# Sixteen-head attention: key products behind the output products, two units ahead, and four small moves on the other engines

## What is computed

```python
q = (hidden_states @ Wq).reshape(B, Sq, H, D)           # H = 16 heads of D = 128, Sq = 512
k = (encoder_hidden_states @ Wk).reshape(B, Skv, H, D)  # Skv = 512, context width 256
v = (encoder_hidden_states @ Wv).reshape(B, Skv, H, D)
q, k = rmsnorm(q, gq), rmsnorm(k, gk)
attn = softmax(einsum('bqhd,bkhd->bhqk', q, k) * scale)
out = einsum('bhqk,bkhd->bqhd', attn, v).reshape(B, Sq, H * D) @ Wo
x = x + tanh(g_xattn[2]) * out
```

```python
def step(state, inp):            # 16 states per channel, 512 positions
    d, b, c, u = inp
    dA = jnp.exp(d[..., None] * A)
    state = state * dA + (d * u)[..., None] * b[:, None, :]
    return state, jnp.einsum('bdn,bn->bd', state, c)
```

## Time and profile before

| | |
|---|---|
| time, median of 3 runs | 3549.21 us (3537.89 to 3550.49) |
| the profiled execution's own time | 3549.66 us |
| its span, first to last instruction | 3547.6 us |
| mean granted TensorE clock | 0.957 |
| busy: PE, DVE, ACT, POOL | 88%, 74%, 51%, 40% of the span |

### The profile page before, as it was taken

How to read it: one execution, slowest core, us unless ns; L and a number is a source line. 1 busy time by engine, 2 the same in 40 slices (tenths; PEclk the granted TensorE clock), 3 DMA queues, 4 the chain that set the end, 5 groups by cost and what they waited for, 6 DMA issues and landing times. The chain is left out here.

```text
span 3547.6 us, 42725 instructions
## 1 busy us (share of the span) xinstructions
PE 3130.4 (88%) x14213; PEld 1831.5 (52%) x14244; DVE 2623.1 (74%) x3494; ACT 1801.9 (51%) x3414; POOL 1416.0 (40%) x956
## 2 busy tenths in 40 slices
PE   7869788999996888699999999999999777998985
PEld 3337544333333555455555555555555356786663
DVE  7855698877765888478777877787777764766886
ACT  5644343666653445465666566655555332664220
POOL 1122288000000000076777777767767544223440
PEclk9879999999998999999999999999999888999997
DMA  4137745222218300255555454445444346665321
GB/s 131 47 117 271 266 121 129 66 57 57 57 30 169 41 1 1 83 175 158 173 172 173 157 172 161 160 157 179 165 158 138 119 166 202 241 249 205 142 72 59
DMA packets 229748, 478.65 MB, mean 135 GB/s; under 512 B 36239, under 2 KB 69647, under 8 KB 213664
## 3 DMA queue, kind: packets, MB, share of 16 engines
q1 hardware_dynamic: 223296, 459.19, 40.9%
q0 software_dynamic: 6240, 16.81, 1.4%
HBM read 387.51 MB, written 92.06 MB: 135 GB/s over the span
## 5 line engine op out<-in xcount | busy, mean ns | idle before, releaser
L2378 POOL TENSOR_TENSOR l2x_inflow<-l2x_dtu,l2x_rows_b 128x512 f32<-128x512 f32 x256 | 419.4, 1638 | 271.2 <-DVE l2x_state L2267 263.0
L178 POOL TENSOR_TENSOR ln_work<-ln_work,minus_half 128x4 f32<-128x4 f32 (+1 forms) x34 | 33.2, 976 | 1037.4 <-DVE ln_work L166 1037.3
L2267 DVE TENSOR_TENSOR_SCAN l2x_state<-l2x_decay,l2x_inflow 128x512 f32<-128x512 f32 x256 | 383.1, 1497 | 16.8 <-ACT l2x_decay L2141 16.8
L1324 DVE TENSOR_REDUCE l1x_mx<-psum 128x2 f32<-128x1024 f32 x256 | 308.3, 1219 | 100.0 <-PE psum L1166 98.5
L2394 POOL TENSOR_TENSOR l2x_y_sum<-l2x_y_sum,l2x_state 128x512 f32<-128x512 f32 x224 | 354.4, 1582 | 33.0 <-DVE l2x_state L2276 33.0
L2076 ACT ACTIVATE l2x_probs<-psum,l2x_soft,l2x_norms 128x512 f32<-128x512 f32 x256 | 195.5, 775 | 320.2 <-DVE l2x_soft L2206 320.2
L1281 ACT ACTIVATE l1x_split<-psum 128x1024 f32<-128x1024 f32 x256 | 262.0, 1025 | 158.7 <-PE psum L1166 158.6
L2276 DVE TENSOR_TENSOR l2x_state<-l2x_state,l2x_rows_c 128x512 f32<-128x512 f32 x256 | 266.8, 1042 | 7.6 <-DMA l2x_rows_c<-l3x_xd_dram 1.1
L126 PE MATMUL psum<-l2x_probs_t,l2x_v_tok 128*128 128x512 f32 x512 | 236.3, 605 | 28.9 <-ACT l2x_probs_t L212 25.9
L126 PE MATMUL psum<-l2x_xt,l2x_wq 128*128 128x512 f32 x512 | 230.9, 594 | 7.7 <-issue 6.2
L126 PE MATMUL psum<-l2x_kt,l2x_qt 128*128 128x512 f32 x512 | 230.5, 593 | 4.0 <-ACT l2x_probs L2076 4.0
(11 more groups left out here) (458 smaller groups left out, 7199.6 us busy)
## 6 DMA issues: line engine op xcount, KB each, us to landing
l2x_rows_b<-l3x_xd_dram SPq DMA_DIRECT2D x256, 256.0 KB, 3.7
l2x_rows_c<-l3x_xd_dram SPq DMA_DIRECT2D x256, 256.0 KB, 3.7
l2w_raw<-l_w SPq DMA_DIRECT2D x38, 1024.0 KB, 7.0
l2x_wkv<-l2x_kv_dram SPq DMA_DIRECT2D x32, 1024.0 KB, 6.9
l2w_raw<-l_w SPq DMA_DIRECT2D x38, 512.0 KB, 4.5
l1x_heads_dram<-l1x_stage SPq DMA_DIRECT2D x32, 512.0 KB, 3.3
l2x_wq<-l_wq SPq DMA_DIRECT2D x16, 1024.0 KB, 7.2
l2x_wo<-l_wo SPq DMA_DIRECT2D x16, 1024.0 KB, 5.3
```

What stands on the lines that cost most here:

```text
L1324: main.drain(dve.tensor_reduce(mx[:, gg % 2, :, j, t], g["psum"][:, b:b + 2, :], AX.X, ALU.max), f"m{n}_0", banks=2)
L2267: dve.tensor_tensor_scan(state[:, s % KEPT, :], decay[:, s % 3, :], inflow[:, s % 3, :], 0.0, ALU.mult, ALU.add).then_inc(scan_done, 1)
L2378: pool.tensor_tensor(inflow[:, s % 3, :], dtu[:], rows_b[:, s % 3, :], ALU.mult).then_inc(inflow_ready, 1)
```

## The change

1. TensorE: the key products move from behind `score(u, 0)` to the end of the iteration, behind the output products, and are those of unit u + 2. The transposes of x move too, to just before the output products, as those of unit u + 2. Both are done once ahead of the loop for unit 0. The list of PSUM jobs follows.
2. ScalarE: squares and copies of the keys move to the end of the iteration in the same way. Two decays come before the first exponentials, the copies of the turned probabilities of head 0 before the first query, and the key scalings are placed anew.
3. VectorE: the maxima and bias of head 1 come before scan 2 instead of before scan 3, those of head 2 before scan 7 instead of before scan 8, and the first value before scan 6 instead of before scan 7. The copies of the turned x go to the iteration's end.
4. GpSimd: the key norms come at the head of an iteration, before step 0's inflow, instead of behind step 3.
5. SyncE: the query weights of unit u + 2 are asked for at step 13 instead of 15.

```diff
--- before.py
+++ after.py
@@ -1792,7 +1792,11 @@
 
 def l2_jobs():
 
-    jobs = []
+    def front(u):
+        turned = [(f"xt{u // G2}_{c}", "act" if c % 2 else "dve") for c in range(DC)] if u % G2 == 0 and u < NU else []
+        return turned, [(f"k{u}_{t}", "act") for t in range(ST)] if u < NU else []
+
+    jobs = front(0)[0] + front(0)[1]
     for u in range(-1, NU):
         pre, on = u + 1 < NU, u >= 0
 
@@ -1808,11 +1812,7 @@
         def query(h):
             return [(f"q{u + 1}_{h}", "act")] if pre else []
 
-        jobs += score(0)
-        if (u + 1) % G2 == 0 and pre:
-            jobs += [(f"xt{(u + 1) // G2}_{c}", "act" if c % 2 else "dve") for c in range(DC)]
-        jobs += [(f"k{u + 1}_{t}", "act") for t in range(ST)] if pre else []
-        jobs += score(1) + query(0) + turn(0) + query(1) + value(0) + turn(1) + score(2) + value(1) + query(2)
+        jobs += score(0) + score(1) + query(0) + turn(0) + query(1) + value(0) + turn(1) + score(2) + value(1) + query(2)
         jobs += turn(2) + score(3) + query(3) + value(2)
         jobs += [(f"ssq{u + 1}", "act")] if pre else []
         jobs += turn(3)
@@ -1820,7 +1820,8 @@
         jobs += value(3)
         jobs += [(f"v{u + 1}_{t}", "act") for t in range(ST)] if pre else []
         jobs += [(f"kt{u + 1}_{h}", "dve") for h in range(4)] if pre else []
-        jobs += [(f"out{u}_{t}", "dve") for t in range(ST)] if on else []
+        turned, keys = front(u + 2)
+        jobs += turned + ([(f"out{u}_{t}", "dve") for t in range(ST)] if on else []) + keys
     return jobs
 
 
@@ -1943,7 +1944,7 @@
                     if n == 6 and u + 1 < NU:
                         ring.wait_filled(sp, 0, f"k{u + 1}_{ST - 1}")
                         value_weight(u + 1)
-                    if n == 15 and u + 2 < NU:
+                    if n == 13 and u + 2 < NU:
                         ring.wait_filled(sp, 0, f"q{u + 1}_3")
                         weight(wq, "l2_wq", u + 2, wq_in)
                     row_b(u * NS + n + 2)
@@ -2038,11 +2039,10 @@
                         ring.fill(transpose_group(pe, bank(f"kt{u}_{h}"), [k_tok[:, t, h * P:(h + 1) * P]
                                                                            for t in range(ST)], g["ident"][:]))
 
+            x_turned(0)
+            context(0, "k", range(ST))
             for u in range(-1, NU):
                 score(u, 0)
-                x_turned(u + 1)
-                context(u + 1, "k", (0, 1))
-                context(u + 1, "k", (2, 3))
                 score(u, 1)
                 query(u + 1, 0)
                 turn(u, 0)
@@ -2062,8 +2062,9 @@
                 value(u, 3)
                 context(u + 1, "v", range(ST))
                 keys_turned(u + 1)
-                output(u, (0, 1))
-                output(u, (2, 3))
+                x_turned(u + 2)
+                output(u, range(ST))
+                context(u + 2, "k", range(ST))
 
         @blk.scalar
         def _(act):
@@ -2141,47 +2142,49 @@
                 act.activation(decay[:, s % 3, :], dt[:, u % 2, :], ACT.Exp,
                                scale=g["a_neg"][:, u % G2, n:n + 1]).then_inc(decay_ready, 1)
 
+            x_turned(0)
+            context(0, "k", k_tok)
             for u in range(-1, NU):
+                decays(u, 0)
+                decays(u, 1)
                 exponent(u, 0)
-                decays(u, 0)
-                x_turned(u + 1)
-                decays(u, 1)
-                context(u + 1, "k", k_tok)
                 decays(u, 2)
                 exponent(u, 1)
                 decays(u, 3)
+                turn(u, 0)
                 query(u + 1, 0)
                 decays(u, 4)
-                turn(u, 0)
                 query(u + 1, 1)
                 decays(u, 5)
                 inverse(u, 0)
-                key_scale(u + 1, 0)
                 decays(u, 6)
                 turn(u, 1)
                 decays(u, 7)
+                key_scale(u + 1, 0)
+                key_scale(u + 1, 1)
                 exponent(u, 2)
                 decays(u, 8)
                 inverse(u, 1)
-                key_scale(u + 1, 1)
                 query(u + 1, 2)
                 decays(u, 9)
                 turn(u, 2)
+                key_scale(u + 1, 2)
                 exponent(u, 3)
                 decays(u, 10)
                 query(u + 1, 3)
-                key_scale(u + 1, 2)
                 decays(u, 11)
                 inverse(u, 2)
-                key_scale(u + 1, 3)
                 decays(u, 12)
                 norm_rows(u + 1)
                 turn(u, 3)
+                key_scale(u + 1, 3)
                 inverse(u, 3)
                 context(u + 1, "v", v_tok)
                 decays(u, 13)
                 decays(u, 14)
                 decays(u, 15)
+                x_turned(u + 2)
+                context(u + 2, "k", k_tok)
 
         @blk.vector
         def _(dve):
@@ -2282,20 +2285,20 @@
                     dve.scalar_tensor_tensor(tile, tile, g["skip"][:, u % G2:u % G2 + 1], y_sum[:, u % 2, :], ALU.mult,
                                              ALU.add).then_inc(y_read, 1)
 
+            x_turned(0)
             for u in range(-1, NU):
                 scan(u, 0)
                 maxima(u, 0)
                 biases(u, 0)
                 gather(u, 0)
                 scan(u, 1)
-                x_turned(u + 1)
                 gather(u, 1)
+                maxima(u, 1)
+                biases(u, 1)
                 scan(u, 2)
                 inverse(u, 0)
                 gather(u, 2)
                 skip_term(u - 1)
-                maxima(u, 1)
-                biases(u, 1)
                 scan(u, 3)
                 gather(u, 3)
                 scan(u, 4)
@@ -2303,13 +2306,13 @@
                 gather(u, 4)
                 scan(u, 5)
                 gather(u, 5)
+                value(u, 0)
                 scan(u, 6)
                 gather(u, 6)
-                value(u, 0)
+                maxima(u, 2)
+                biases(u, 2)
                 scan(u, 7)
                 gather(u, 7)
-                maxima(u, 2)
-                biases(u, 2)
                 scan(u, 8)
                 gather(u, 8)
                 inverse(u, 2)
@@ -2395,10 +2399,10 @@
 
             for u in range(-1, NU):
                 for n in range(NS):
+                    if n == 0:
+                        key_norms(u + 1)
                     inflows(u, n)
                     add_state(u, n - 1)
-                    if n == 3:
-                        key_norms(u + 1)
                     if n == 13 and u % G2 == 1:
                         ln.pool(pool, u // G2)
                     if n == 12:
```

## The result

The changed kernel takes 3558.82 us (median of 20 runs, 3552.14 to 3568.43) against 3539.79 us for the kernel before in the same comparison (20 runs, 3528.15 to 3556.12). The ratio is 1.0053, 95% interval 1.0041 to 1.0064: slower by 0.53%, some 19 us. The forecast was + 34 us. It was added to a kernel before of 3549.21 us, the median of three runs; over twenty runs that kernel takes 3539.79, 9.4 us less.

The account below looks back on a forecast made before the run. TensorE was taken to bound the attention stage, with VectorE's chain to turn 2 without slack. Regular units + 52, x + 2, layer norms − 18, start + 3, last unit − 5: + 34 us, 3583 us (+ 0.95%), range 3512 to 3608.

Parts of the forecast that it names:

- Lost cover: With score 1 directly behind score 0, VectorE idles 4 to 5 us during the key products, before maxima 0.
- VectorE's new order: Earlier maxima 1, value 0 and maxima 2 are free; scan and gather 7 leave the chain to turn 2, −3.21 us.
- Key norms at the head: GpSimd's norms wait until t = 2.1, delay inflow 2 and the last sum to 6.5; no idle time until past 30.
- Chain from score 0 to turn 2: In a regular unit, 34.05 us plus port waits (+4.0, less 0.8 and 0.7), together 36.5 us; bounds 34.05 and 37.3.
- After turn 2: Rest of a regular unit, 41.39 us before; exponent 3 and query 3 come later, a new stall of 0.7 us.
- Start: Unit 1's key products can't hide their weight load behind score 0 any more: + 3 us.
- Last unit: The unit without key or query products gets shorter by 3.21 and 1.36 us: − 5 us.
- Layer norms: VectorE's lateness after a layer norm falls in the 5.99 us ahead of score 0: 4.56 us saved four times, − 18.
- Units with x: Three units turning x: 1.74 us of extra work had cost only 1.03, the rest lay in the old hole; + 2.
- Nothing to speak of: Rival, chance 0.22: GpSimd catches up during the maxima, chain 34.05 to 35.2 us, no query 3 stall; about 3546 us.
- Faster: Rival, chance 0.22: TensorE stays the bound, VectorE's chain to turn 2 under 32.1 us, 42 us less, 3507 us.
- Slower still: Rival, chance 0.10: holes before turn 2 also cost TensorE its clock, 1.7 us in each of fifteen units, 3609 us.

Follow-up runs that it names:

- short sums: The changed kernel with 14 of a unit's 15 GpSimd state sums cut to 8 of 512 columns (sums left incomplete): 3502.28 us, one run.

## Why the prediction was right in kind and wrong in size

The change came out slower, at the low end of what was forecast (+ 19 of + 34 us, within the range of 3512 to 3608). Of the 24.2 us between 3583 and 3558.82, 9.4 lie in the median of three runs that it started from. I go through its steps.

*Lost cover.* Right as a cause: VectorE's idle time was 4.57 us (4 to 5 forecast), and the move of the keys is the largest single piece, 4.0 us a unit with VectorE's old order. But 1.6 of these are TensorE's lower clock behind a hole that the changed kernel doesn't have.

*VectorE's new order.* Right in sign. It gives back 2.6 us once the keys are moved (85.1 to 82.5), and costs 1.4 without that.

*Key norms at the head.* Priced through the port waits. It costs 83.97 − 82.5 = 1.5 us, or 2.0 with VectorE's order of before (85.1 to 87.1). In this order the three pieces lead from the unit before to the changed one, 81.1 + 4.0 − 2.6 + 1.5 = 84.0, as each is the difference of two neighbouring runs. By TensorE's busy time in the windows, idle time makes + 2.3, − 1.4 and + 1.4 of them, and slower or faster matmuls + 1.6, − 1.1 and 0. Against the norms behind step 3 at a granted clock of 1.00 (81.9), the head costs 2.1.

*Chain from score 0 to turn 2: 36.5 forecast, 36.15 measured.* The sum was near, its parts were not all right. Of four port waits three came (gather 2, bias 1, scan 3), 3.0 us in place of 4.0. Gather 3 took 0.69 us undisturbed, since GpSimd had run out of work behind scan 3. Gather 1 took 1.57, a wait that I hadn't counted, 0.9 us. Scan 2 and scan 6 gave back 1.5, as in the sum, and the start of the chain another 0.3. So 2.1 us came on top of 34.05 where the sum has 2.5. They depend on GpSimd's load: with short sums the chain is 33.40.

*The holes.* I had put some 3 us among head 2's scores and 1 before turn 2. They were 0.73 and 0.57, with 0.66 and 1.04 before them: the same lateness was met earlier, in smaller pieces. I had not read the wait of value 0 through the order in which ScalarE empties the banks.

*After turn 2: 0.7 forecast.* The hole at the query-norm product is 1.15 us, but the old 0.21 ahead of the norm transposes went, and the key products follow the output products 0.4 us sooner than score 0 did. From turn 2 to the next key products the unit takes 41.82 us against 42.1 in the sum.

*The step that failed: the size of the regular unit, 84.6 us against 83.97.* The chain is high by 0.35, which is the term of the port waits, and the rest of the unit by 0.3; the keys are exact at 6.00. Fourteen units multiply this to 8.7 us: 23.8 measured over the 14 distances where 32.5 was forecast. With 3.2 us of the first unit and 1.0 of the last, these are the 13 us between + 34 and the stage's + 21. The prediction's own sign says the same: it called itself wrong if GpSimd had idle time between its norms and maxima 2, for then the port waits were counted wrongly. GpSimd had 1.16 us. It is a mis-sized term and not a wrong mechanism.

*Start: + 3, and + 3.5 for the first unit.* Measured + 3.3 for both. The key weights' load did show (a wait of 3.10 us), but the hole at the norm transposes shrank from 1.74 to 0.72, since ScalarE's last key scaling now stands behind the norm rows: + 2.1. The unit itself lost only 1.2. It has no sum of a unit before to close, an operation of 1.75 us on VectorE, and its chain from score 0 to turn 2 takes 34.47 us instead of 36.15. That is 3.2 us of the overestimate.

*Last unit: − 5.* Its chain from score 0 to turn 2 fell from 38.62 to 33.58, by 5.0 as forecast; from the last query norms to the stage's end it is − 6.0. *Layer norms: − 18.* Right: that unit now takes what a regular unit takes (83.96 and 83.98). *Units with x: + 2.* Their extra is 1.74 us, all of it now. Right.

The sum of what was measured: + 3.3 + 23.8 − 6.0 = + 21.1, the stage's + 21.0.

*The rivals.* "Nothing to speak of" fell by its size: a regular unit gains nothing and loses 2.9 us, though half of its claim held, in that GpSimd did catch up once, behind scan 3. "Faster" needed a chain under 32.1 us. Even with short sums it is 33.40, since the 1.04 us hole stays; but the relief of the port gives 37.5 us (3539.79 to 3502.28) where that rival had 42, so the port is what keeps the change from gaining. "Slower still" fell here: the granted clock stayed at 1.00 in all units, and no hole of a regular unit passed 1.16 us. Its mechanism is real where holes are longer. Behind those of 4.26 and 6.14 us the same four transposes took 1.11 us instead of 0.66, and a unit's matmuls took 1.2 to 2.5 us longer than in the kernel before, about what that rival priced (1.7). Behind 2.37 us the clock fell in some units and stayed in others.

*GpSimd.* I had said that it would have no idle time for 25 us. It had a short one, 1.16 us, waiting for scan 3, and gather 3 profited: the port waits behind it were fewer than counted.

**What stays open.** The three shares of a unit come from mean distances in single profiles, good to some 0.3 us, and they are not fully additive (the norms' place costs 1.5 or 2.0), in part because the granted clock differs between these runs. ScalarE's new order and the earlier load of the query weights were never run apart from the move of the keys, so their share of the 4.0 us is not shown. I didn't try other places for the norms with maxima 3 early, nor value 0's wait without the dependence on query 0.

## What to carry to other kernels

A product that seems to lie idle in the middle of a chain may be the cover under which another engine does its work. Ask of each moved piece what ran beneath it, and price that first (4.0 us a unit here, of which 1.6 were slower matmuls behind the new hole). On two engines that slow each other, look for an operation that leaves the other undisturbed, here the long power on few elements, and place it beside the other engine's dense work, not beside its waits. Before naming a hole, look up which instruction stands behind it and which one ends it: the two largest holes here stood ahead of turn 0 and waited for head 1, where the sum of the chain looks at head 2. And when a hole moves as something is moved ahead, measure the chain from end to end. Moving maxima 3 left it alone twice (53.75 and 53.88, 51.89 and 52.04 us) and shortened it once (51.87 to 50.73), and only the last was a gain.

## What the runs showed of the hardware that I had not expected

A GpSimd power of 128x16 took 3.70 us and left scans and gathers beside it undisturbed (1.24, 1.22 and 0.69 us), whereas a 128x512 product beside a scan made it 2.28. The Trainium skill, "SBUF — State Buffer", section "Who interferes with whom", calls the shared port pair an exclusive lock, the loser waiting for the whole operation. The trace has the scan longer by 1.07 us beside operations that take 1.27 alone, in this kernel as before. That is near the rule, with about 0.2 us of overlap. The power's rows don't agree with it: the power reads SBUF too and lasts 3.70 us, and a gather and a scan issued during it took 0.69 and 1.22 us, as if alone. Here the measurement decides.

A tiny VectorE product on 128x4 takes 1.18 us when a product of GpSimd holds the port, and 0.16 otherwise. A bias is thus as dear as a scan's wait if it falls badly.
